# Down weights of the experts: from the sync queue to the scalar engine's queue

## What is computed

```
def _mlp(x, gw, uw, dw):
    return jax.nn.silu(x @ gw.T) * (x @ uw.T) @ dw.T
x = hidden_states.reshape(B * S, H)                       # 512 tokens, H = 512
rw = _route(x, gate_w, gate_bias)                         # 8 of 64 weights per token
expert_out = jax.vmap(lambda gw_, uw_, dw_: _mlp(x, gw_, uw_, dw_))(Wg, Wu, Wd)   # I = 352
routed = jnp.einsum('eth,te->th', expert_out, rw)
shared = _mlp(x, Sg, Su, Sd)
out = (routed + shared).reshape(B, S, H)
```

## Time and profile before

| | |
|---|---|
| three runs | 1879.22, 1879.92, 1888.1 us; median 1879.92 us |
| profiled execution, own time | 1885.62 us |
| its span, first to last instruction | 1883.8 us |
| mean granted TensorE clock | 0.952 of full |
| busy: PE, PE weight loads, DVE, ACT, POOL | 1733.8, 1387.1, 963.0, 620.0, 453.9 us |
| stage of the experts' tiles | about 298 to 776 us of the span |
| DMA in slices 7 to 16 of 40 (47 us each) | 298 to 350 GB/s; over the whole span 119 GB/s |

### The profile page before, as it was taken

The page is one execution under the profiler, slowest core; times in us unless marked ns, Lnnn a source line. Parts: engine busy times, 40 slices in busy tenths (PEclk is TensorE's granted clock), DMA queues, the critical chain, the costliest instruction groups (busy, mean ns, idle before and its releaser), DMA issues. The chain is left out here.

```text
span 1883.8 us, 34953 instructions
## 1 busy us (share of the span) xinstructions
PE 1733.8 (92%) x13132; PEld 1387.1 (74%) x13133; DVE 963.0 (51%) x2045; ACT 620.0 (33%) x848; POOL 453.9 (24%) x430
## 2 busy tenths in 40 slices
PE   8767799999999999879999999999999999997975
PEld 3545567777777777758888888888888888984452
DVE  2534675666666666444544444444444544444265
ACT  1111114655555555203424223242332424221110
POOL 2010005555555555410302103030120302100100
PEclk9787899999999999989999999999999999998977
DMA  7000228999999999600202002020100202002000
GB/s 280 0 1 1 106 77 298 350 344 343 342 339 335 344 340 338 199 0 2 71 6 71 6 1 71 6 71 6 51 26 1 71 6 71 1 16 105 22 1 22
DMA packets 67605, 223.27 MB, mean 119 GB/s; under 512 B 8914, under 2 KB 26578, under 8 KB 57376
## 3 DMA queue, kind: packets, MB, share of 16 engines
q1 hardware_dynamic: 53152, 196.29, 29.2%
q0 software_dynamic: 14336, 25.19, 6.3%
HBM read 208.07 MB, written 21.76 MB: 122 GB/s over the span
## 5 line engine op out<-in xcount | busy, mean ns | idle before, releaser
L1065 PE MATMUL PS<-S_r 128*128 128x256 f32 x2496 | 335.1, 289 | 19.5 <-issue 13.3
L1065 PEld LDWEIGHTS PS<-S_r 128*128 128x128 f32 x2496 | 310.6, 192 | 47.2 <-issue 38.8
L1056 PE MATMUL PS<-S_r 128*128 128x384 f32 (+1 forms) x1536 | 314.2, 355 | 0.0
L1510 PE MATMUL PS<-S_r,R_r 128*128 128x352 f32 x1152 | 298.1, 349 | 1.7 <-DVE R_r L1636 1.7
L1056 PEld LDWEIGHTS PS<-S_r 128*128 128x128 f32 x1536 | 273.2, 192 | 11.0 <-issue 3.1
L1510 PEld LDWEIGHTS PS<-S_r,R_r 128*128 128x128 f32 x1152 | 198.7, 188 | 20.8 <-issue 18.6
L1211 ACT COPY S<-PS 128x512 f32<-128x512 f32 (+1 forms) x128 | 64.4, 503 | 299.2 <-PE PS L1100 299.2
L1002 POOL COPY S<-qbd 128x128 f32 (+1 forms) x32 | 9.4, 295 | 634.3 <-PE PS L1083 613.3
L1264 DVE CUSTOM_DVE_ANT_0 R<-PS,maskadd 128x384 f32<-128x384 f32 (+1 forms) x256 | 136.2, 570 | 29.4 <-PE PS L1083 27.2
L1246 DVE TENSOR_TENSOR R<-PS,vbias 128x256 f32<-128x256 f32 (+1 forms) x208 | 88.2, 424 | 120.3 <-PE PS L1065 116.2
L1533 PE MATMUL PS<-R 128*128 128x512 f32 (+1 forms) x288 | 133.4, 599 | 5.3 <-DVE R L1646 4.8
(11 more groups left out here) (258 smaller groups left out, 2538.1 us busy)
## 6 DMA issues: line engine op xcount, KB each, us to landing
R<-in_w_gu SPq DMA_DIRECT2D x34, 1408.0 KB, 19.3
R<-in_w_dna SPq DMA_DIRECT2D x50, 512.0 KB, 17.5
qbd<-in_w_gu SPq DMA_DIRECT2D x16, 1408.0 KB
S<-in_w_gu SPq DMA_DIRECT2D x16, 1408.0 KB
S<-in_ctxT SPq DMA_DIRECT2D x24, 768.0 KB
R<-in_w_dnb SPq DMA_DIRECT2D x50, 192.0 KB, 18.3
xnT<-in_w_dna SPq DMA_DIRECT2D x16, 512.0 KB
S<-in_ctxT SPq DMA_DIRECT2D x8, 898.0 KB
```

The source lines that it names most:

```text
L1056: last = nc.tensor.matmul(PS[:, bank, 0:n], w3[0][:, cc, f0:f0 + P], x3[i][:, cc, 0:n], start=(cc == 0 and w3 is wkv_hi and x3 is ctx_hi), ...
L1065: last = nc.tensor.matmul(PS[:, bank, 0:256], x3[need][:, cc, k0:k0 + P], w3[1][:, cc, f0:f0 + 256], start=(cc == 0 and w3 is wkv_hi and x ...
L1510: last = nc.tensor.matmul(PS[:, gu, 0:I], x3[:, c, :], w3[:, c, gu, :], start=(c == 0 and x3 is hi[0] and w3 is hi[1]), stop=(c == NC - 1 ...
```

## The change

`load` on SP returns, in all rounds but the first, after the gate and up weights. A new `load_down` on ACT reads the expert number into a register of ACT and issues the two DMAs of the down weights on ACT's own DMA queue. It stands directly behind `rows_out_copy` of the tile whose down weights lay in that buffer, and waits for nothing of its own: `rows_out_copy` has waited for `y_made` of that tile. In the last round it is called once, for place 3.

```diff
@@ SP, load(r, k)
                     if not isinstance(r, int):
-                        sp.wait_ge(y_made, i - NBUF + 1)
-                    elif k == 1:
+                        return
+                    if k == 1:
                         sp.wait_ge(sh_u, 2 * NT)
                     elif k >= 2:
                         sp.wait_ge(sh_d, 2 * NT + k - 3)
@@ ACT
+                def load_down(r, k):
+
+                    e = act.value_load(eot_row[0:1, column(r, k)], min_val=0, max_val=E - 1)
+                    ev = bass.ds(e, 1)
+                    act.dma_start(wdn[k][:, 0:2, :].rearrange("p c n -> p (c n)"),
+                                  a["w_dna2"][ev, :, :].rearrange("e p n -> (e p) n")).then_inc(w_dn[k], 16)
+                    act.dma_start(wdn[k][0:96, 2, :],
+                                  a["w_dnb"][ev, :, :].rearrange("e p n -> (e p) n")).then_inc(w_dn[k], 16)
+
                 def step(r, k, final=False):
                     silu(r, k)
                     if not (final and k == NBUF - 1):
...
                     if not (isinstance(r, int) and r == 0 and k == 0):
                         rows_out_copy(*tile_before(r, k))
+                        if not (final and k):
+                            load_down(*(tile_before(r + 1, k) if k else (r, NBUF - 1)))
```

## The result

The changed kernel takes 1870.88 us (median of 6 runs, 1865.19 to 1872.86), the kernel before, on the same chip, 1881.62 us: ratio 0.9933, 95% interval 0.9911 to 0.9954. The profiled execution took 1871.98 us (span 1870.2) against 1885.62. It is faster by 0.67%, the interval runs from 0.46% to 0.89%: clear of zero, with its lower end just under the 0.5% that the prediction took as what a measurement of this kernel can tell. Every ratio here counts only executions within 1.5% of the fastest of their kernel.

The account below looks back on a forecast made before the run. The prediction took DMA to bound the expert-tile stage, 7.5 us per tile against PE's 7.20. A 4 us gain from earlier gate and up weights, all costs 0, gave 1879.9 - 4 = 1875.9 us, range 1865 to 1889.

Parts of the forecast that it names:

- the 4 us: Expert-tile stage: gain taken for SP issuing gate and up weights earlier, between bounds of 0 and 5.8 us.
- same: Outcome class: time within about 0.5%, 9.4 us, of no change, which a measurement cannot tell apart; chance 0.71.
- the third queue lifts the rate: Rival for the expert-tile stage: three queues reach 355 GB/s, all 15.0 us of waits go, 1864.9 us; chance 0.17.
- First, order: 4.8 us: SP's queue: gate and up weights land earlier while down weights slip by 2.3 steps of 2.1 us, gained once.
- The gap at the start, 1.0 us: Window 308 to 312 us, engines at 0.80 while SP waits for the first tile's product: 1.0 us of transfers can move there.
- Upper bound 5.8 us: Most that SP's earlier issue of gate and up weights could gain, from transfer order and the gap at the start.
- ACT's new work, cost 0: ACT's register load and two issues per tile take 1.9 us, covered by idle time and 0.7 us of slack; cost 0.
- Down weights later, cost 0: Down weights issued behind ACT's copy go out 3.9 us later, out of 16.8 us to spare; cost 0.
- SP issues within 1 us of PE's change: Sign that the forecast is right: SP issues gate and up weights within 1 us of PE going over to the down product.
- Late gathers: Rival: POOL's gathers slow by 3.8 us as a third queue takes turns, 22 us over 62 steps, 1902 us; chance 0.12.
- ACT as bound: Rival: ACT's issues cost 3.3 us or more per tile, over 7.7 us per step, 16 us and more, 1896 us; chance 0.04.
- The context for the next layer: On SP's queue it moves ahead of the last tiles' down weights; cost 0 and no gain.

Follow-up runs that it names:

- the kernel without the third part: Kernel before without the 192 KB fetch of each tile's last 96 rows of down weights from round 1 on: 1867.88 us, ratio 0.9928.
- the kernel with only this part on ACT: Kernel before with only the 192 KB, 96-partition fetch of down weights moved to ACT's queue from round 1 on: 1866.09 us, ratio 0.9909.
- the wide one: Kernel before, all weights on SP, the 192 KB down-weight fetch read as 128 rows instead of 96 from round 1 on, contents scrambled: 1866.82 us, ratio 0.9914.
- order alone: Kernel before, all on SP's queue, each tile's gate and up weights issued ahead of the previous tile's down weights: 1881.13 us, ratio 0.9988.
- SP's wait put back: Changed kernel, but SP again waits for the down product of the tile four back before the next tile: 1870.44 us, ratio 0.9943.
- 256 KB more: One extra 256 KB fetch per tile on the down weights' queue: kernel before 1928.26 us, changed kernel 1905.78, kernel before with all fetches 128 partitions wide 1887.71.

## Why the prediction was right or wrong

**The time** was close: forecast 1875.9 (1865 to 1889), measured 1870.88. That is luck, for the reason was wrong: the 4 us stood for a cause that turned out to be worth nothing, and the gain between the medians is 10.7 us, outside the 1 to 7 us of the forecast itself. The measured time lies in the range because the range reached down to a rival. The gain is 0.67% where I gave "same" 0.71, and by its mechanism the case that came out is that rival, "the third queue lifts the rate", chance 0.17.

**What bounds the kernel**: right. 7.5 us of DMA against 7.20 of PE, 15.0 us of waits: the kernel without the third part, the kernel with only this part on ACT and the wide one all step at 7.20 us and save 14 to 17 us by their ratios. They come within 1 to 3 us of that rival's forecast of 1864.9 us (1866 to 1868).

**First, order: 4.8 us**: wrong, about 0 (ratio 0.9988 with order alone; the full gain with the old order and a wide fetch). With order alone the head start does come, 24 steps without waits in place of 10, but it is gone by the end of the stage, where only the rate counts. The 16.8 us to spare may be too high as well. I wrote that no row tells when down weights land, but the page has medians for those in R over all issues, 17.5 and 18.3 us; by the first of these the ones issued at 555.02 would land at 572.5 and not 566.1, with 10.4 us to spare, and the term would be 3.0 us. For that step itself it stays open, since the weights issued behind them were in by 570.33.

**The gap at the start, 1.0 us**: no run shows it apart, and with SP's wait put back the gain is the same.

**"Upper bound 5.8 us"**: this is the step that failed. It rested on "the engines are already at 103.8%". The share is the time that packets take, whatever they move in it: 342, 351, 356 and 373 GB/s were all measured at 103 to 104%, and 200 GB/s at 105%. "The engines show no idle time that a queue could fill" was true and no argument. The right bound was the 15.0 us of waits, of which the change took 11.8. I also had a rate to compare with, slices of 350 GB/s, and named it without weighing it.

**The rule of the Trainium skill** that I put beside this term ("DMA: Bandwidth & Descriptors", Rules for kernel authors: spreading DMAs over queues does not help bandwidth) does not hold here: 342 to 356 GB/s with the same bytes, both DMA-bound. One queue with every fetch 128 partitions wide reaches more than either, 373 GB/s.

**ACT's new work, cost 0**: right. I had estimated 1.9 us; the second issue ends 0.92 us behind the copy, and silu starts when PE lets it, since the register load runs beside the copy. **Down weights later, cost 0**: right, 13.9 us to landing in the median for the third part and no wait for them in the changed kernel; with 256 KB more they became what PE waits for (14.3 us). **SP issues within 1 us of PE's change**: right, 473.92 against 473.59; worthless all the same.

**Late gathers**: right in kind, small in size. Three waits of 2.7 us in all, not 22 us: they make most of the difference between the change's 7.25 us and 7.20, 3.3 us over the stage. **ACT as bound**: did not occur; in the step shown the issues took 0.34 and 0.35 us, and none in the stage over 0.46. (ACT's 4.35 us and 3.3 us make 7.65, not "over 7.7": that rival's price is 14 us and not 16.) **The context for the next layer**, cost 0: no run shows it apart.

## What to carry to other kernels

Busy DMA engines are not engines at their limit: compare GB/s at equal share between stretches, and when a stage is held by DMA take all its waits as the upper bound. Look for the one fetch that covers fewer than 128 partitions, and see whether it can be laid out over all of them, before moving fetches to other queues. No run here did that with its numbers in their right places: the product takes the third part as 96 rows on 96 partitions, so that layout would have to change as well. To compare two ways of fetching, add bytes until both are held by DMA; where PE is the bound, they all look equal.

## What the runs showed of the hardware

All of this is from 330 to 750 us of one core's stage. Two fetches of 64 partitions in place of one of 128 brought the rate from 342 to 200 GB/s, at full share. One fetch of 192 KB, as 96 rows of 2048 B or as 128 rows of 1536 B, among 2.82 MB per tile, made the difference between 342 and 373 GB/s on one queue. Two queues deliver differently in the same busy time: in the changed kernel with 256 KB more, SP's queue with only 11 KB rows moved 76.47 MB in 44.1% of the engines' time, 25.8 GB/s per engine, and ACT's queue with rows of 2 and 4 KB, the narrow fetch among them, 52.03 MB in 36.3%, 21.3 GB/s. And a register load with an issue behind it on ACT came out 0.07 us behind the activation ahead of it, so the load cost nothing there.
